# Three DRAM buffers of a graph kernel laid out in another order

## The reference

```python
node_i, node_j = node_features[i_idx], node_features[j_idx]        # i = src, j = dst
h = relu(concat([node_i, node_j, edge_features]) @ mW1 + mb1)      # 53,125 x 512
aggregated = segment_sum(h @ mW2 + mb2, i_idx)                     # per source node
u = relu(concat([node_features, aggregated]) @ uW1 + ub1)
x = x + node_features + u @ uW2 + ub2
```

## Time and profile before

| | |
|---|---|
| median of 3 runs | 3069.82 us (3068.47 to 3076.61) |
| the profiled execution | 3078.97 us, of which its span 3077.2 us |
| mean granted TensorE clock of it | 0.873 |
| busy share: PE, DVE, POOL, ACT | 83%, 65%, 58%, 25% |
| DMA | 399.80 MB, mean 130 GB/s |

### The profile page before, as it was taken

How to read it: one execution, slowest core, us unless ns; L and a number is a source line. 1 busy time by engine, 2 the same in 40 slices (tenths; PEclk the granted TensorE clock), 3 DMA queues, 4 the chain that set the end, 5 groups by cost and what they waited for, 6 DMA issues and landing times. The chain is left out here.

```text
span 3077.2 us, 33769 instructions
## 1 busy us (share of the span) xinstructions
PE 2559.4 (83%) x8467; PEld 1467.8 (48%) x8467; DVE 1992.4 (65%) x4427; ACT 777.1 (25%) x2019; POOL 1795.9 (58%) x1837
## 2 busy tenths in 40 slices
PE   5488887599999999899889777777787777777799
PEld 2144443255555555466666434444444434443577
DVE  8999999477777777634555544444445444444798
ACT  1011110376767677512223100000010000000232
POOL 5777777766767666521010477777746777777300
PEclk8699998699999999989999877777777787877799
DMA  9223224299999999841100233333334333333101
GB/s 285 62 82 94 80 78 155 71 268 262 264 264 268 258 264 263 250 157 52 33 26 1 88 106 105 105 106 105 106 91 135 106 105 106 105 105 105 34 1 43
DMA packets 191742, 399.80 MB, mean 130 GB/s; under 512 B 41450, under 2 KB 83964, under 8 KB 191358
## 3 DMA queue, kind: packets, MB, share of 16 engines
q0 software_dynamic: 93888, 248.27, 29.7%
q1 hardware_dynamic: 95632, 147.24, 14.4%
q10 hardware_dynamic: 2032, 2.13, 0.2%
HBM read 295.16 MB, written 104.50 MB: 130 GB/s over the span
## 5 line engine op out<-in xcount | busy, mean ns | idle before, releaser
L1590 POOL DMA_INDIRECT nbr_yg<-y_d,gidx x878 | 830.1, 945 | 268.6 <-PE nbr_sum L1657 142.8
L1657 PE MATMUL nbr_sum<-nbr_yg,nbr_hot 128*128 128x258 f32 x1756 | 737.2, 538 | 267.8 <-DMA nbr_yg<-y_d,gidx 225.2
L1616 DVE TENSOR_TENSOR nbr<-nbr_sum,nbr 128x258 f32 x878 | 373.7, 426 | 595.6 <-PE nbr_sum L1657 511.6
L1657 PEld LDWEIGHTS nbr_sum<-nbr_yg,nbr_hot 128*128 128x128 f32 x1756 | 377.3, 251 | 616.0 <-DMA nbr_yg<-y_d,gidx 227.8
L771 POOL DMA_INDIRECT qg<-q_d,rb x480 | 478.6, 997 | 210.4 <-DVE hb L857 118.2
L393 POOL DMA_INDIRECT recs_d<-recs,slot_src x416 | 403.7, 970 | 149.3 <-issue 130.5
L888 PE MATMUL p_sum<-hb,wide 128*96 128x512 f32 x960 | 452.3, 593 | 2.9 <-ACT hb L817 2.8
L817 ACT ACTIVATE hb<-hb 128x512 f32<-128x512 f32 x480 | 296.2, 630 | 208.5 <-DVE hb L857 204.6
L857 DVE TENSOR_TENSOR hb<-p_h,qg 128x512 f32<-128x512 f32 x480 | 311.0, 680 | 31.6 <-DMA qg<-q_d,rb 28.7
L614 PE MATMUL acc<-col_hot,lane_hot 128*128 128x440 f16 x832 | 197.0, 399 | 99.7 <-DVE lane_hot L567 99.7
L843 DVE SCALAR_TENSOR_TENSOR agg<-agg,keep,p_sum 96x512 f32<-96x512 f32 x240 | 178.2, 743 | 130.9 <-PE p_sum L888 130.4
(11 more groups left out here) (285 smaller groups left out, 3146.0 us busy)
## 6 DMA issues: line engine op xcount, KB each, us to landing
agg_d<-agg SPq DMA_DIRECT2D x240, 192.4 KB, 5.1
nbr_yg<-y_d,gidx POOLq DMA_INDIRECT x878, 2.7
p_low<-p_d SPq DMA_DIRECT2D x11, 768.0 KB, 12.4
recs_d<-fill SPq DMA_DIRECT2D x16, 510.0 KB, 16.8
rb<-recs_d SPq DMA_DIRECT2D x60, 136.0 KB
qg<-q_d,rb POOLq DMA_INDIRECT x480, 5.7
recs_d<-recs,slot_src POOLq DMA_INDIRECT x416
agg_d<-no_sums SPq DMA_DIRECT2D x1, 6540.8 KB, 48.3
```

The costliest lines, as they stand in the source:

```text
L1590: pool.indirect_dma_start(yg[t % YB][:, 0:D], None, S.y[:, :], bass.IndirectOffsetOnAxis(ap=C.gidx[:, t:t + 1], axis=0)).then_inc(s_gath[t ...
L1616: dve.tensor_tensor(nbr, p_sum[t % SUMS][:, 0:W], nbr, ALU.add).then_inc(s_acc, 1)
L1657: pe.matmul(p_sum[t % SUMS][:, 0:W], hot[t // BT % HOTS][:, t % BT, :], yg[t % YB][:, :], start=True, stop=True).then_inc(s_sum, 1)
```

## The change

Three of the buffers get other places. No shape, no instruction, no queue and no wait changes.

```diff
         S.recs = dram("recs_d", [NSLOTS + BLOCK, REC])
-        S.xn, S.y = (dram(f"{n}_d", [NPAD, D]) for n in ("xn", "y"))
-        S.p, S.q = dram("p_d", [(NBS + 1) * P, HID]), dram("q_d", [NPAD, HID])
+        S.xn = dram("xn_d", [NPAD, D])
+        S.y = dram("y_d", [NPAD, D])
         S.agg = dram("agg_d", [(NBS + 1 + NGS) * SB, HID + 1])
+        S.p = dram("p_d", [(NBS + 1) * P, HID])
+        S.q = dram("q_d", [NPAD, HID])
         S.u = dram("u_d", [HID, NPAD])
```

## The result

The changed kernel takes 3140.64 us in the median (3133.61 to 3144.39, 4 runs), the kernel before 3070.74 us. The ratio is 1.0218, 95% interval 1.0203 to 1.0233: 2.2% slower, where no change was forecast. The instructions of every engine are the same in both. The compiled program has the buffers where the prediction put them: agg_d at 15,130,624, p_d at 69,107,712, q_d at 78,020,608, u_d unmoved.

What follows compares the result with a forecast made beforehand. The prediction took PE to bound the edge stage, with DMA close behind, and POOL the first stage. All its terms were 0 us, so the forecast was no change: a median of 3069.8 us, range 3060 to 3082.

Steps and rivals of the forecast that it cites:

- What bounds the kernel: Edge stage, 686 us: PE sets the pace, DMA close behind; first stage: POOL's scatters, after 11.4 us waiting for first_rows.
- Addresses: Whole program: agg_d goes where P was, P and Q move up 53,977,088 bytes, alignment and instructions stay; 0 us.
- Writes and reads of the sums: Edge and node stages: PE waits for no slab write and 9.7 us for the loads; 0 us.
- First fills: First stage: fills of agg_d and P's attribute rows write the same bytes elsewhere; 0 us, at most 9.0 us won.
- Gathers of Q: Edge stage: 480 gathers in random order don't care where Q begins; 0 us, faster ones give at most 2.8 us.
- Rival 1: Edge stage: gathers slow down at Q's new distance from the slabs, DMA bounds; 20% slower adds 22 us; chance 0.08.
- the spare: Edge stage: the typical gather lands 0.86 to 1.47 us early; slower landing costs nothing until 0.86 us is used up.
- the 15%: Edge stage: gathers' 69.4% of the DMA engines can grow by some 15% until the share's sum is 1.03.
- Rival 3: Whole program: the order of the calls does not set the addresses, nothing moves, 3069.8 us; chance 0.03.
- The profiled execution: Whole program: the profile of the changed kernel should lie 9.1 us above its median, at 3079 us.

Runs made afterwards that it cites:

- before_256k: Kernel before with an unused buffer of 262,144 bytes ahead of the sums, P and Q unmoved: 3448.59 us against 3405.99, ratio 1.0113.
- p_agg_q: Kernel before with its buffers in the order P, sums, Q (sums at 24.0 MB, Q at 78.0 MB): 3166.05 us, ratio 1.0303.
- shift_all: Kernel before with P, Q and the sums all 53,977,088 bytes further on, behind an unused buffer: 3072.26 us against 3073.3, ratio 1.0003.
- agg_q_p: Kernel before with its buffers in the order sums, Q, P (sums at 15.1 MB, Q at 69.1 MB): 3139.48 us, ratio 1.0192 to the kernel before.
- agg_gap_pq: Changed kernel with P and Q 53,977,088 bytes further behind the sums (Q at 132.0 MB): 3145.21 us, ratio 1.0223 to the kernel before.
- all_256k: Kernel before with all seven buffers 262,144 bytes further on, inputs and output unmoved: 3449.67 us, ratio 1.0004.
- sums_away: Kernel before with only the sums 53,977,088 bytes further on, at 84.6 MB, P and Q as before: 3072.35 us, ratio 0.9992.
- small_gap_after: Changed kernel with an unused buffer of 2,359,296 bytes ahead of the sums, moving sums, P and Q: 3072.14 us, ratio 0.9988 to the kernel before.
- before_512k: Kernel before with an unused buffer of 524,288 bytes ahead of the sums: 3406.19 us, ratio 0.999.
- recs_256k: Kernel before with records, P and Q 262,144 bytes further on and the sums 524,288: 3441.32 us, ratio 1.0002.
- after_wide_rows: Changed kernel with 2176 bytes of room for each row of the sums instead of 2052: 3444.58 us, ratio 0.9971 to the kernel before.
- before_wide_rows: Kernel before with 2176 bytes of room for each row of the sums: 3072.97 us, ratio 0.9995.
- after_odd_rows: Changed kernel with 2140 bytes of room for each row of the sums: 3074.21 us, ratio 0.9998 to the kernel before.

## Why the prediction was wrong

- **What bounds the kernel** was right: PE in the edge stage with DMA close behind, and POOL in the first stage behind first_rows. The loss is in the edge stage, in the waits for gathers that the prediction watched; that the first stage takes a part of it is not shown.
- **Addresses** were right to the byte, and "Term: 0 us" did not follow. The rule that the prediction took from the Trainium skill (DMA: Bandwidth & Descriptors, "How a descriptor splits into AXI transactions") holds for rows of 2048 bytes, but was told too widely: a short row off its boundary, 96 bytes in the section's table, needs no more transactions than one on it. It played no part here, and no run shows it. Equal rows at equal offsets from a boundary of 2048 bytes were taken for equal cost.
- **The step that failed** is "Writes and reads of the sums ... Term: 0". I looked at who waits for the slabs (nobody), not at what the slabs do to the transfers beside them. Moving only the sums, by 256 KiB, brings 1.1% (before_256k) with P and Q where they were, and another 256 KiB takes it away. With the slabs at some places the gathers of Q cost 73 us of engine time for a MB instead of 62, while the packets of the hardware queue, the slabs among them, go from 46.1 to 47.4.
- **First fills**: "writes in long runs over megabytes meet every part of the memory wherever they begin" failed as a reason for equal cost: the fill landed after 68.2 us instead of 48.3. Nor is it one long run: as L310 is written, it goes through the 34 slabs row by row, a row of each in turn, 196,992 bytes apart. I had priced slower fills, at 1.2 us for a tenth. At 41% that makes 4.9 us, and 3.5 us more of waiting were measured, but p_agg_q, with a still slower fill, waits only 0.5 us more than before. The agreement of the price may be luck.
- **Gathers of Q**: "Rows in random order over 6.5 MB should not care where the 6.5 MB begin" held over megabytes (shift_all, agg_q_p, agg_gap_pq). The gathers are what gets dearer, and the slabs' place decides whether. That Q's own fine place has a part in it, once the slabs lie badly, is not ruled out (all_256k).
- **Rival 1** had the right place and sign, at a chance of 0.08, and the wrong cause: another distance between the two streams costs nothing (sums_away), and the distance of the changed kernel costs nothing at another place (small_gap_after). Its price was too small for what was seen. By its formula a median landing of 6.7 us is 0.14 us beyond the spare, 11 us; 54 were measured. The landings spread (11.6 us at most instead of 8.3), and each late one is waited for, while an early one gives nothing back. The engines' account fits better: 73.1 / 61.9 = 1.18 times the gathers' time is past the 15% from which the engines are full, and the share did read 0.97.
- **Rival 3** was wrong: the order of the lines sets the addresses.
- **The profiled execution** was expected 9.1 us above the median, as in the kernel before; it lies 7.0 us below it. The other slow kernels with the sums at 15.1 MB spend 738.0 and 750.4 us from the first to the last gather, so part of the 15 us between the traces and the medians may be the edge stage's too; no trace settles it.

**The cause, as far as it was shown.** It is the places of the slabs in memory. That the base of the sums counts is shown: before_256k against before_512k for the stage, and all_256k against recs_256k for the fills. That the pitch of 196,992 bytes is the other half is shown for the fills: on one chip, with the base at 440 KiB modulo 512 KiB, they take 67.3 us for a MB with it (all_256k) and 48.1 with 208,896 (after_wide_rows). For the gathers it is likely and not shown without a rival. With a pitch of 205,440 or 208,896 bytes they take 55 us for a MB at the bad base. But in these two kernels Q moved as well, to 116 and 16 KiB modulo 512 KiB, and on neither chip was a kernel run that loses time. At the good base, with Q unmoved, the wider pitch makes them cheaper too (54.1 instead of 61.9, before_wide_rows). The alignment of the rows has no visible part: on the same chip the hardware queue takes 46.5 us for a MB with rows at 2140 bytes and 46.6 at 2176. 196,992 is 3 x 65,536 + 384, so eight slabs on, a slab lies 3 x 524,288 + 3072 bytes further: the slabs go round the same eight places modulo 512 KiB and drift by 3 KiB a round. A pattern that holds over a stage and shifts slowly with the group would fit the falling GB/s of the changed kernel; this is argued, not shown.

**What stays open.** Which bits of an address matter. The base 256 KiB further visits the same eight places four slabs later, so the place modulo 512 KiB can't be the whole of it. Fifteen of the sixteen other kernels with this pitch in the table agree with it by the ratio; all_256k does not, though its engine time rises by part of the loss and its fills agree. Two runs are missing: the changed kernel with only Q moved by 256 KiB, and the changed kernel and its wide-pitch version side by side on one chip. Whether engines collide at one part of the memory was argued from the pitch, and no run shows it. The Trainium skill (DMA: Bandwidth & Descriptors, "Latency and other measured facts") tells of copies that lose up to half their rate at row pitches of large powers of two, restored by 4 KiB more of pitch and not by 192 bytes. The runs here may be of its kind: 384 bytes beside a multiple of 64 KiB go with a loss, 8832 bytes (after_odd_rows) with none. That the base of the buffer decides whether such a pitch hurts is not in that rule.

## What to carry to other kernels

Where the DMA engines are nearly full (a share of 0.93 here), a buffer's DRAM address can be a parameter of the time. When only declarations change, look at the pitch of every slab-wise write: here one 384 bytes beside a multiple of 64 KiB went with a time that depends on where the buffer lies. Try some more room for the rows (here 4% more memory); at the two bases where it was tried, nothing was lost. Judge a write stream by what it does to its neighbours' engine time, not only by who waits for it; and price a slower gather by its tail and the engines' share, not by its median.

## What the runs showed of the hardware

- Moving the sums by 262,144 bytes (before_256k) brought 1.1% of time, with no instruction changed; on that chip the gathers took 73.4 us of engine time for a MB, and 62.9 with another 262,144 bytes.
- The same 6.5 MB fill landed after 43.0, 48.3, 68.2 or 74.0 us (after_odd_rows, before, after, p_agg_q), as the sums' base and pitch went.
- At 263 GB/s the DMA share of the edge stage was 0.93 (before) or 0.85 (before_wide_rows), with only the pitch of the sums between them: the share is engine time, and says how hard the bytes come, not how many.
